# Moving a coupling cycle ahead of two expert steps in a pipelined decoder kernel

## The chip, the cores and the metric

The kernel runs on one core of one Trainium2 chip. The time is device microseconds (us) of one execution; of several runs the median is given. Lower is better.

## What is computed

The reference runs 32 sequences of 256 tokens of width 256 through six sublayers. Each adds its result to its input and takes a layer norm, and each reads the output of the one before:

```python
x = _layernorm(x + _L0_attn_ref(x, ...))        # random features, exp
x = _layernorm(x + _L0_xattn_ref(x, ctx, ...))  # cross attention, 16 heads, 120 keys
x = _layernorm(x + _L0_ffn_ref(x, ...))         # three coupling cycles
x = _layernorm(x + _L1_attn_ref(x, ...))        # state-space scan, 512 channels x 16 states
x = _layernorm(x + _L1_xattn_ref(x, ctx, ...))  # gated, gelu
x = _layernorm(x + _L1_ffn_ref(x, ...))         # 8 experts, the best one is taken
```

The two sublayers that matter here are the third and the sixth. The third is a small network with gelu that yields a gate for each token, and the gate turns the token's vector; this is done three times, the second cycle on the result of the first:

```python
for _ in range(NUM_CYCLES):
    tf = _coupling_net(out, ...)           # three gelu layers and a sigmoid
    combined = 0.7 * gf + 0.3 * tf         # gf: the same for a whole sequence
    coupling = BASE_COUPLING + adaptive_range * (combined - 0.5) * 2.0
    out = out + coupling * _twist(out)
```

In the sixth, the kernel lets all eight experts compute each token and adds the results with weights, of which all but one are zero.

## The kernel before

Two sequences, 512 tokens, make a group; there are 16. The kernel is a pipeline written out by hand: for each engine there is one list of work for a **turn**, and in a turn four groups are at different places. `f` is in the front part (sublayers 1 to 3), `m` in the scan of sublayer 4, `b` in the back part (5 and 6), and `nxt` is the one whose first sublayer and keys are made ready. 18 turns run: two that fill, 13 in a loop with all four groups present, one without `nxt`, one with `m` and `b` alone, and one with `b` alone. An engine works its list strictly in the order in which it stands in `turn` (TensorE) or `turn_` (VectorE, ScalarE, GpSimd, called POOL in the profile), so an instruction that waits holds up all that stands behind it on its engine.

**The coupling cycles.** `cycle(f, s)` on TensorE issues layers 1 to 4 for the two sequences of the group (the first layers of cycle 0 are issued just ahead of it by `layer(f, 1, 0)` and `layer(f, 1, 1)`, with the steps of the small global network, `glob`, between). ScalarE applies a gelu behind each layer (L1416, L1420, L1424) and the gate (L1430), after it has loaded the table for gelu (L1498). VectorE's `rotate` (L1038 to L1043) turns the vectors with the gate, and the next cycle's first layers wait for that. Layer 1 of cycle 0 waits for the copies of the second norm, which ScalarE makes in `copy_and_sum` (L1372).

**The experts.** `experts(b, s0, s1)` on TensorE issues expert steps `s`; a step is one block of 128 tokens through two experts: a 128x512 result in PSUM bank `MB[s % 2]`. `combine(b, s0, s1)` on VectorE (L1199) adds the results: for each pair of steps four sums, expert one of both blocks, then expert two of both. There are 16 steps. Since they use only two banks, step `s` waits until both sums of step `s - 2` are done:

```python
if s >= 2:
    pe.wait_ge(expert_added.sem, expert_added.at(g, added_after(s - 2)))
```

Steps 0 and 1 wait for the start of the sum. On its side a sum waits for its step's matmuls.

**The scan.** 64 scans (16 states for each of four chunks of channels; L1087) run on VectorE, with four outputs between (L1093). `states(m, n)` advances this list to entry `n`; scan 33, the first of the third chunk, is entry 34. ScalarE makes the decays for the scans (`decays`, L1479), at most 12 ahead of VectorE; POOL adds the states (L1671). At the first scan of a chunk VectorE also waits for a square that ScalarE makes (L1474).

`keys(nxt, f)` and `values(nxt, f)` on TensorE prepare the next group's attention; VectorE's `values` adds their bias (L982).

TensorE's matmuls are recorded under the line of one helper, L535 (transposes: L413 and L719), so the operands tell them apart: `w_expert_w,x45T` is an expert step, `x12T,w_cn_w` layer 1 of a cycle, `spare,w_cn_w` layers 2 to 4, `g,w_gc_w` the global network. A float32 matmul is recorded twice, so a step of two matmuls counts x4.

Of the kernel before, what the change touches and what calls it, by code (L numbers as in the profile page):

```python
# [136 lines left out]
def program(nc, ins, out):  # L137
    nc.disable_value_cache = True
    with ExitStack() as ctx:
# [293 lines left out]
        def added_after(s):  # L433


            return 4 * (s // 2) + 3 + s % 2
# [96 lines left out]
        def _(pe):  # L533
# [261 lines left out]
            def experts(g, s0, s1):  # L795

                for s in range(s0, s1):
                    pair, t = s // NT, s % NT
                    if s >= 2:

                        pe.wait_ge(expert_added.sem, expert_added.at(g, added_after(s - 2)))
                    else:
                        pe.wait_ge(acc_start.sem, acc_start.at(g, 2))
                    for c in range(DC):
                        last = mm(MB[s % 2][:, :], n5.xT[:, c, t * P:(t + 1) * P],
                                  expert_w[:, c, pair * 2 * D:(pair + 1) * 2 * D], c == 0, c == DC - 1)
                    last.then_inc(expert_ready.sem, 1)
# [10 lines left out]
            def turn(f, m, b, nxt):  # L818
# [66 lines left out]
                    experts(b, 0, 2)  # L885
                if f is not None:
                    norm_turn(pe, n2, f, TURN)
                if b is not None:
                    experts(b, 2, 4)
                if f is not None:  # L890
                    layer(f, 1, 0)
                    glob(f, 1)
# [6 lines left out]
                    keys(nxt, f)  # L899
                    values(nxt, f)  # L900
                if b is not None:
                    experts(b, 4, 9)
                if f is not None:
                    cycle(f, NB)
                if b is not None:
# [23 lines left out]
            with pe.Fori(0, G - 3) as i:  # L929
                turn((i, 2), (i, 1), (i, 0), (i, 3))  # L930
# [6 lines left out]
        def _(v):  # L937
# [160 lines left out]
            def states(g, upto):  # L1098

                if g is None:  # L1100
                    return
                if scanned.n is None:
                    scanned.start(v, g)
                while scanned.n < upto:
                    step(g, *PLAN[scanned.n])
                if upto == len(PLAN):
                    scanned.end()
                    scanned.n = None
# [74 lines left out]
            def combine(g, s0, s1):  # L1183

                for s2 in range(s0 // 2, s1 // 2):
                    pair, t0 = s2 // 2, s2 % 2 * 2
                    for e in range(2):
                        for t in (t0, t0 + 1):
                            s = pair * NT + t
                            done = 4 * s2 + 2 * e + (t - t0)  # L1190
                            if e == 0:
                                v.wait_ge(expert_ready.sem, expert_ready.at(g, s + 1))

                            if e:
                                v.wait_ge(expert_added.sem, expert_added.at(g, done - 1))
                            elif pair:
                                v.wait_ge(expert_added.sem, expert_added.at(g, done - 5))
                            x = 2 * pair + e
                            v.scalar_tensor_tensor(out=acc[:, t, :], in0=MB[s % 2][:, e * D:(e + 1) * D],  # L1199
                                                   scalar=weight[:, t, x:x + 1], in1=acc[:, t, :], op0=ALU.mult,  # L1200
                                                   op1=ALU.add).then_inc(expert_added.sem, 1)
# [21 lines left out]
            def turn_(f, m, b, nxt):  # L1223
# [44 lines left out]
                    norm_apply(v, n2, f)  # L1268
                if b is not None:
                    combine(b, 0, 2)  # L1270
                states(m, 30)
                if b is not None:
                    combine(b, 2, 4)
                states(m, 32)
                if f is not None:
                    global_base(f)
                    rotate(f, 0)
                    rotate(f, 1)
                states(m, 34)
                if b is not None:  # L1280
                    combine(b, 4, 6)
                states(m, 36)
# [490 lines left out]
```

## Time and profile before

| | |
|---|---|
| median of 3 runs | 3106.39 us (3101.62 to 3107.36) |
| profiled execution | 3099.29 us |
| its span, first to last instruction | 3097.5 us |
| mean granted TensorE clock | 0.872 |
| TensorE matmuls busy | 82% |
| VectorE busy | 81% |
| ScalarE busy | 56% |
| POOL busy | 48% |

The profile is of one execution. A line of its timeline has the start, the busy time, the engine and the source line, what is written from what, and how many instructions were merged into the line; in brackets stands how long the engine was idle just before and which instruction ended that. Merged instructions overlap a little, so the start of the next line is the better measure of how far one has come. Ends of matmuls are modelled.

### The profile page before, as it was taken

Reading aid. Unit: us, or ns where it says so; the run is one execution under the profiler, and the core shown is the slowest. Engines: PE = TensorE matmul, PEld = TensorE weight load, DVE = VectorE, ACT = ScalarE, POOL = GpSimd, SP = SyncE. Lnnn points to the kernel's source line nnn. Section 1 sums busy time; section 2 is a strip of 40 time slices with the busy share of each in tenths; the row PEclk is TensorE's granted clock in tenths of the full one; section 3 lists DMA queues with packets and bytes.
Section 4 is the critical chain, followed back from the end, with each engine's and each line's share of the span. In section 5 each row is a group of like instructions: output and inputs, shape, how many; then the busy total and the mean of one; then the engine's idle time right before and its main releaser. Section 6 shows DMA issues by size and latency. Waiting matters only on the chain.

```text
span 3097.5 us, 41602 instructions
## 1 busy us (share of the span) xinstructions
PE 2540.1 (82%) x11020; PEld 1469.9 (47%) x11020; DVE 2495.3 (81%) x4288; ACT 1727.8 (56%) x3062; POOL 1487.4 (48%) x1159
## 2 busy tenths in 40 slices
PE   6896888979888897888988788888888889887556
PEld 3544554544444454445545444554544445454323
DVE  2368888897978889898888978788897888978783
ACT  1457564646657474665646466564656646465620
POOL 1046354554535455563545545354553545456460
PEclk7868888888989989999898899898898989978687
DMA  3000000000000000000000000000000000000000
GB/s 131 10 8 10 14 11 14 17 14 7 10 21 10 14 17 14 7 10 21 10 14 13 18 7 10 21 10 14 13 3 21 10 14 7 7 7 1 14 7 7
DMA packets 16849, 45.72 MB, mean 15 GB/s; under 512 B 2248, under 2 KB 7056, under 8 KB 16400
## 3 DMA queue, kind: packets, MB, share of 16 engines
q1 hardware_dynamic: 16656, 43.96, 4.2%
q14 instruction: 171, 1.40, 0.2%
q8 instruction: 22, 0.36, 0.1%
HBM read 35.57 MB, written 8.39 MB: 14 GB/s over the span
## 4 chain that ended last, share of the span: by engine, by line
PE 47%; DVE 28%; issue 14%; ACT 7%; DVEq 2%; POOL 1%; ACTq 0%; DMA 0%; SPq 0%; POOLq 0%
PE bank L535 45%; DVE h_ring L1087 14%; DVE x L1199 3%; DVE ln_stats L387 2%; DVE smax L991 1%; POOL ysum L1671 1%; ACT a_ring L1479 1%; DVE x L405 1%; DVE xpad L1093 1%; PE bank L413 1%; DVE soft L1066 1%; ACT L1485 1%; ACT L1339 1%; DVE ln_mv L391 1%; ACT spare L1420 1%
## 5 line engine op out<-in xcount | busy, mean ns | idle before, releaser
L1671 POOL TENSOR_TENSOR ysum<-ysum,h_ring 128x512 f32<-128x512 f32 x896 | 1155.2, 1289 | 633.3 <-DVE h_ring L1087 571.3
L1087 DVE TENSOR_TENSOR_SCAN h_ring<-a_ring,bank 128x512 f32<-128x512 f32 x1024 | 1172.7, 1200 | 27.2 <-ACT bank L1474 16.2
L1479 ACT ACTIVATE a_ring<-soft,decay 128x510 f32<-128x510 f32 x1024 | 675.7, 717 | 198.4 <-DVE h_ring L1087 198.0
L535 PE MATMUL bank<-w_expert_w,x45T 128*128 128x512 f32 x1024 | 541.1, 675 | 199.0 <-DVE x L1199 191.4
L535 PEld LDWEIGHTS bank<-w_expert_w,x45T 128*128 128x128 f32 x1024 | 213.2, 216 | 490.9 <-DVE x L1199 253.5
L1658 POOL TENSOR_TENSOR soft<-xc,soft 128x512 f32<-128x512 f32 x64 | 81.0, 1276 | 655.2 <-ACT soft L1457 655.2
L535 PE MATMUL bank<-x3T,w_winT 128*128 128x512 f32 x512 | 291.0, 704 | 39.7 <-ACT x3T L419 31.4
L991 DVE TENSOR_REDUCE smax<-bank 128x4 f32<-128x480 f32 x256 | 156.4, 652 | 143.1 <-PE bank L535 143.1
L535 PE MATMUL bank<-qT,kmask 32*120 32x256 f32 x1024 | 207.2, 497 | 50.2 <-ACT spare L1386 40.6
L535 PE MATMUL bank<-spare,w_cn_w 128*128 128x256 f32 x768 | 217.7, 408 | 37.0 <-ACT spare L1416 22.4
L1199 DVE SCALAR_TENSOR_TENSOR x<-bank,weight,x 128x256 f32<-128x256 f32 x512 | 212.5, 474 | 40.4 <-PE bank L535 40.4
L398 ACT ACTIVATE ln_logv<-ln_mv,eps 128x4 f32<-128x4 f32 x96 | 28.3, 295 | 330.5 <-DVE ln_mv L391 252.7
L535 PE MATMUL bank<-kmask,qT 32*128 32x240 f32 x1024 | 151.8, 417 | 46.1 <-DVE smax L991 45.2
L1386 ACT ACTIVATE spare<-bank 120x512 f32<-120x512 f32 x256 | 138.4, 593 | 81.5 <-PE bank L535 81.4
L535 PEld LDWEIGHTS bank<-x3T,w_winT 128*128 128x128 f32 x512 | 104.3, 220 | 165.1 <-issue 111.5
L535 PEld LDWEIGHTS bank<-spare,w_cn_w 128*128 128x128 f32 x768 | 131.8, 193 | 105.7 <-ACT spare L1416 37.3
L535 PE MATMUL bank<-x12T,w_cn_w 128*128 128x256 f32 x768 | 180.0, 384 | 2.3 <-ACT x12T L1372 2.3
L1671 POOL TENSOR_TENSOR ysum<-h_ring 128x512 f32<-128x512 f32 x64 | 81.3, 1270 | 197.5 <-DVE h_ring L1087 197.5
L413 PE MATMUL bank<-w_ident,x 128*128 128x128 f32 x640 | 127.4, 322 | 49.6 <-DVE x L405 45.6
L535 PEld LDWEIGHTS bank<-x12T,w_cn_w 128*128 128x128 f32 x768 | 146.0, 192 | 40.3 <-issue 20.1
L1416 ACT ACTIVATE spare<-bank,w_columns 128x256 f32<-128x256 f32 x192 | 80.5, 472 | 139.6 <-PE bank L535 139.3
L535 PEld LDWEIGHTS bank<-kmask,qT 32*128 32x128 f32 x1024 | 94.9, 198 | 129.5 <-DVE smax L991 83.8
(149 smaller groups left out, 3890.2 us busy)
## 6 DMA issues: line engine op xcount, KB each, us to landing
x0T<-in_xT SPq DMA_DIRECT2D x16, 512.0 KB, 3.3
x<-in_x SPq DMA_DIRECT2D x16, 512.0 KB, 4.3
out<-x SPq DMA_DIRECT2D x16, 512.0 KB, 3.0
ctxT<-in_ctxT SPq DMA_DIRECT2D x16, 240.0 KB, 2.5
ctxTb<-in_ctxT SPq DMA_DIRECT2D x16, 240.0 KB, 2.7
ctxb<-in_ctx SPq DMA_DIRECT2D x16, 240.0 KB, 3.0
w_expert_w<-in_expert_w SPq DMA_DIRECT2D x1, 2048.0 KB
w_winT<-in_winT SPq DMA_DIRECT2D x1, 1024.0 KB
```

The source lines that it names most:

```text
L387: n.chain.then(v.bn_stats(n.stats[:, t, :], n.sum[:, t, :]))
L391: last = v.bn_aggr(n.mv[:, t, :], n.stats[:, t, :])
L413: last = pe.transpose(banks[c][:, t * P:(t + 1) * P], n.x[:, t, c * P:(c + 1) * P], ident[:, :])
L535: return pe.matmul(o, l, r, start=start, stop=stop)
L991: v.tensor_reduce(smax[:, t, :].rearrange("p (e r h) -> p r e h", e=DC, r=4)[:, r, :, :], bank[u % 3][:, 0:480].rearrange("p (e h k) -> p ...
L1087: scanned.then(v.tensor_tensor_scan(h_ring[:, k % HRING, :], a_ring[:, k % RING, :, :].rearrange("p b s -> p (b s)"), xc2, 0.0, ALU.mult, ...
L1199: v.scalar_tensor_tensor(out=acc[:, t, :], in0=MB[s % 2][:, e * D:(e + 1) * D], scalar=weight[:, t, x:x + 1], in1=acc[:, t, :], op0=ALU.mu ...
L1386: a.activation(probs[:, s % 4, :, :].rearrange("p k s -> p (k s)"), bank[s % 3][0:KEYS, :], ACT.Exp, scale=1.0 / np.sqrt(DK)).then_inc(pro ...
L1416: a.activation(h1[:, b, r, :], bank[b][:, r * S:(r + 1) * S], ACT.Gelu, bias=col("cn_b1", r)).then_inc(l1_ready.sem, 1)
L1479: a.activation(a_ring[:, k % RING, :, 1:S], delta[:, c, :].rearrange("p (b s) -> p b s", b=NB)[:, :, 1:S], ACT.Exp, scale=decay[:, k:k + 1 ...
L1658: p.tensor_tensor(out=delta[:, c, :], in0=xc[:, c, :], in1=soft[:, c, :], op=ALU.add)\
L1671: p.tensor_tensor(out=total, in0=first, in1=h_ring[:, k % HRING, :], op=ALU.add)\
```

## The change

On TensorE expert steps 2 and 3 no longer stand between the transposes of the second norm and the first layers of cycle 0. They are issued behind cycle 0 and the next group's keys and values, in one run with steps 4 to 8. On VectorE the four sums of steps 2 and 3 move from behind scan-list entry 30 to behind entry 34, which stands behind the rotations of cycle 0; the sums of steps 4 and 5 then follow behind entry 35 instead of directly behind entry 34. Entries 31 and 32 follow entry 30 without a break. No instruction is added or removed, and the lists of ScalarE, POOL and the DMA queue are as they were.

```diff
@@ TensorE, turn @@
                 if f is not None:
                     norm_turn(pe, n2, f, TURN)
-                if b is not None:
-                    experts(b, 2, 4)
                 if f is not None:
                     layer(f, 1, 0)
                     glob(f, 1)
...
                     keys(nxt, f)
                     values(nxt, f)
                 if b is not None:
-                    experts(b, 4, 9)
+                    experts(b, 2, 9)
                 if f is not None:
                     cycle(f, NB)
@@ VectorE, turn_ @@
                 if b is not None:
                     combine(b, 0, 2)
-                states(m, 30)
-                if b is not None:
-                    combine(b, 2, 4)
                 states(m, 32)
                 if f is not None:
                     global_base(f)
                     rotate(f, 0)
                     rotate(f, 1)
                 states(m, 34)
+                if b is not None:
+                    combine(b, 2, 4)
+                states(m, 35)
                 if b is not None:
                     combine(b, 4, 6)
                 states(m, 36)
```

## Rows read from the trace of the kernel before

**Rows 1.** The page: span, and busy time of each engine.
```profile
span 3097.5 us, 41602 instructions
...
PE 2540.1 (82%) x11020; PEld 1469.9 (47%) x11020; DVE 2495.3 (81%) x4288; ACT 1727.8 (56%) x3062; POOL 1487.4 (48%) x1159
```

**Rows 2.** Chain of waits, 1494 to 1545 us: start, length (both us), who.
```profile
1500.93 10.25 PE bank L535 x40
...
1536.37 0.42 DVE couple L1038
```

**Rows 3.** Timeline of TensorE, turn around 1500 us: start, us, line, operands, count.
```profile
1500.93 3.70 PE L535 MATMUL bank<-w_expert_w,x45T 128*128 128x512 f32 x8 [0.38 <-DVE x L1199]
...
1508.46 0.28 PE L535 MATMUL bank<-g,w_gc_w 128*64 128x2 f32 x2
1508.67 1.13 PE L535 MATMUL bank<-spare,w_cn_w 128*128 128x256 f32 x4
...
1516.88 3.60 PE L535 MATMUL bank<-w_expert_w,x45T 128*128 128x512 f32 x8
1521.77 3.70 PE L535 MATMUL bank<-w_expert_w,x45T 128*128 128x512 f32 x8 [1.30 <-DVE x L1199]
1526.54 1.98 PE L535 MATMUL bank<-w_expert_w,x45T 128*128 128x512 f32 x4 [1.07 <-DVE x L1199]
```

**Rows 4.** Timeline of ScalarE in the same turn.
```profile
1501.56 3.78 ACT L1479 ACTIVATE a_ring<-soft,decay 128x510 f32<-128x510 f32 x6
1505.36 1.28 ACT L1498 ACT_TABLE_LOAD   x1
1506.65 0.84 ACT L1416 ACTIVATE spare<-bank,w_columns 128x256 f32<-128x256 f32 x2
1507.38 0.26 ACT L1400 ACTIVATE g<-bank,w_columns 128x2 f32<-128x2 f32 x1
1508.57 0.84 ACT L1416 ACTIVATE spare<-bank,w_columns 128x256 f32<-128x256 f32 x2 [0.92 <-PE bank L535]
```

**Rows 5.** Timeline of VectorE in the same turn.
```profile
1506.75 1.64 DVE L1199 SCALAR_TENSOR_TENSOR x<-bank,weight,x 128x256 f32<-128x256 f32 x4
...
1513.41 0.41 DVE L1038 TENSOR_SCALAR couple<-gate,gate_scale,base 128x256 f32<-128x256 f32 x1 [2.44 <-ACT gate L1430]
...
1519.34 1.22 DVE L1087 TENSOR_TENSOR_SCAN h_ring<-a_ring,bank 128x512 f32<-128x512 f32 x1 [0.88 <-ACT bank L1474]
1520.48 1.63 DVE L1199 SCALAR_TENSOR_TENSOR x<-bank,weight,x 128x256 f32<-128x256 f32 x4
...
1525.61 1.27 DVE L1199 SCALAR_TENSOR_TENSOR x<-bank,weight,x 128x256 f32<-128x256 f32 x3 [0.22 <-PE bank L535]
1526.79 2.32 DVE L1087 TENSOR_TENSOR_SCAN h_ring<-a_ring,bank 128x512 f32<-128x512 f32 x2
...
1536.37 0.41 DVE L1038 TENSOR_SCALAR couple<-gate,gate_scale,base 128x256 f32<-128x256 f32 x1 [0.80 <-ACT gate L1430]
```

**Rows 6.** VectorE in other turns; engines and clock (PEclk, after POOL) in two stretches.
```profile
1335.34 0.41 DVE L1038 TENSOR_SCALAR couple<-gate,gate_scale,base 128x256 f32<-128x256 f32 x1 [2.44 <-ACT gate L1430]
...
1699.54 0.41 DVE L1038 TENSOR_SCALAR couple<-gate,gate_scale,base 128x256 f32<-128x256 f32 x1 [2.44 <-ACT gate L1430]
...
410.00:448.00 38.00, 34.97 (x123) 21.15 (x121) 32.22 (x52) 29.10 (x58) 19.57 (x16) 1.00 0.06 21
...
2593.00:2631.00 38.00, 34.97 (x123) 21.32 (x122) 32.22 (x52) 28.70 (x58) 19.25 (x15) 1.00 0.00 0
```

**Rows 7.** Timeline of TensorE: pairs of expert steps after stops, last turns.
```profile
2801.23 6.05 PE L535 MATMUL bank<-w_expert_w,x45T 128*128 128x512 f32 x8 [4.50 <-DVE x L1199]
...
2954.79 5.40 PE L535 MATMUL bank<-w_expert_w,x45T 128*128 128x512 f32 x8 [3.42 <-DVE x L1199]
...
2984.64 3.70 PE L535 MATMUL bank<-w_expert_w,x45T 128*128 128x512 f32 x8 [2.73 <-DVE x L1199]
```

**Rows 8.** Timeline of ScalarE in the first turn behind the loop.
```profile
2788.17 0.84 ACT L1416 ACTIVATE spare<-bank,w_columns 128x256 f32<-128x256 f32 x2 [0.60 <-PE bank L535]
```

## The prediction

> **What bounds the kernel now.** I read the page first: TensorE is busy for 82% and VectorE for 81% of the span [rows 1], so neither share settles anything. The order of work repeats every turn (some 180 us), so I took the turn around 1500 us and read its chain of waits: from 1500.93 to 1536.37 us the chain runs almost wholly through TensorE, with short visits to ScalarE and VectorE [rows 2]. It ends at the rotation of the second cycle, which VectorE waits for. From there VectorE works nearly without a gap to the end of the turn, so what delays that rotation delays the turn, and the next one starts behind it. So I followed the stretch engine by engine.
>
> In that stretch VectorE is idle four times: 2.44 us before the first rotation, 0.88 us before scan 33 of the list, 0.22 us before the second sum of the pair of expert steps 6 and 7, and 0.80 us before the second rotation, 4.34 us in all [rows 5]. The same waits stand in all 13 loop turns, to within 0.01 us; the first rotation of two more turns is shown [rows 6]. One turn can thus be worked out and multiplied.
>
> **The change part by part.**
> *What is removed at the old place.* Expert steps 2 and 3 (the "third and fourth") are eight matmuls, 3.70 us on TensorE from 1500.93 us [rows 3]. Their four sums are one 1.64 us group at 1506.75 us, 1.55 us up to the next scan [rows 5]. Taking the sums out there wins nothing: VectorE then meets its 2.44 us wait for the first gate 1.55 us earlier and waits longer. No transfer moves, and nothing moves past anything on SP's or POOL's queue.
>
> *What the first cycle gains.* The copies of the second norm end about when ScalarE turns to its decays, 1501.56 us [rows 4]; the first layer can start then instead of after the two expert steps, some 2.7 us earlier. But ScalarE is not there yet: six decays (3.78 us) and a table load stand ahead of the first gelu, which starts at 1506.65 us with no wait [rows 4]. It cannot move. Only the second gelu can: it waits 0.92 us for TensorE [rows 4]. Without that wait the next limit is TensorE's second layer of the small global network, which needs the activation that starts at 1507.38 us and takes 0.26 us [rows 4]; so it starts at about 1507.70 instead of 1508.46 us, and layer 2 behind it at 1507.91 instead of 1508.67 us [rows 3]. **The whole first cycle, and with it the rotation, the keys and the values, comes 0.76 us earlier.** Bounds: nothing (if TensorE keeps its place) and 0.92 us (the whole wait). I take 0.76, as the row that becomes late next is in the trace.
>
> A rule to weigh here: the row puts the next gelu 1.29 us after the start of the table load. The Trainium skill (ScalarE: Activation LUTs, What ACT_TABLE_LOAD costs) counts about 2.66 us for a switch, a drain included; by it the first gelu would come at about 1508.0 us, the gain would be nil and the sum some 10 us larger. This trace disagrees with the page, and I go by the row.
>
> *What is added behind the cycle.* TensorE now issues steps 2 to 8 in one row where it issued 4 to 8. All use two PSUM banks: step s waits for both sums of step s-2. So TensorE and VectorE take turns, and a pair has a period that the trace shows: step 6 starts at 1521.77, step 8 at 1526.54 us, 4.77 us, of which 3.70 us are matmuls and 1.07 us the wait for VectorE [rows 3]. From the first pair to the second it is 1521.77 - 1516.88 = 4.89 us. In the old order steps 4 and 5 found their banks long free, as the sums of 2 and 3 had been done before the rotation. In the new order steps 4 and 5 must wait for those sums.
>
> Laid out: values end 0.76 us earlier, so step 2 starts at 1516.12 us. The scan before the sums shifts from 1519.34 to 1518.58 us, so the moved sums start at 1519.72 us (old: the next pair's at 1520.48 us [rows 5]) and just meet the end of step 3. Step 4 starts 1.29 us after that, 1521.01 us; step 6 at 1525.78, step 8 at 1530.55 us, against 1526.54 us before. **One more period of 4.77 less the 0.76 gained: 4.01 us later.**
>
> VectorE agrees. Its old wait of 0.22 us at the second sum of a pair becomes a wait at both later pairs, since between two pairs it has only its sums (1.55 us) and one scan (1.2 us) against 4.77 us, at the last pair also the value copies. The scan behind the pair of steps 6 and 7 moves from 1526.79 [rows 5] to about 1530.80 us. The second cycle stands behind step 8 on TensorE, and ScalarE's last decay ahead of that cycle needs that very scan; both come 4.0 us later, so the 0.80 us wait stays as it is and the second rotation starts at about 1540.4 us.
>
> *What hides it afterwards.* Nothing that I find: the later waits of TensorE are for VectorE, and ScalarE's and POOL's hang on scans; all move along. What is queued behind the waiting step 4 on TensorE is steps 5 to 8 and the whole second cycle; behind VectorE's waiting sums stand all later scans.
>
> *The two turns behind the loop.* The first has no next input, so no keys and values; its second gelu waits only 0.60 us [rows 8], so the gain is 0.76 - 0.32 = 0.44 and the loss 4.33 us. The second has no front part and no cycle: the sums move behind scan 33 and this arrives 1.55 us earlier, but one more period follows and starts cold, since TensorE then has stood for over 8 us. The nearest rows for a pair after a long stop are 5.40 us (3.42 us stop) and 6.05 us (4.50 us stop) [rows 7], against 3.60 us [rows 3]: 4.77 + 1.80 - 1.55 = 5.0 us, or 5.7 by the other row. I take 5.0. The first two turns and the last have the same order in effect.
>
> *The sum.* 13 x 4.01 = 52.1, with 4.3 and 5.0: 61.4 us. The profiled execution took 3099.29 us; with the change about 3160.7. The median of the runs is 7.1 us higher, so on that scale 3167.8; I say 3166.
>
> The bounds: without any gain 13 x 4.77 and the two turns, 71 us; with the full 0.92 us 59 us. The clock outside the stretch differs from turn to turn anyhow (the first rotation, at 1335.34, 1513.41 and 1699.54 us, shows turns of 178.1 and 186.1 us [rows 5, 6]), and every later stage now falls elsewhere in that pattern: I allow 15 us down and 25 us up for it.
>
> **The rivals.**
> *A, my forecast: one more turnaround of the two banks in each turn.* 3166 us, chance 0.73.
>
> *B, the clock falls as well.* Over the stretch the granted clock is 1.00 (2.4 GHz) in all 13 turns, first and last shown [rows 6]; the waits of 1.30 and 1.07 us between pairs do not lower it, nor does one of 2.73 us, while pairs after stops of 3.42 and 4.50 us run slow [rows 7]. The new order adds stops of about 1.2 us ahead of the first layer and 2 us ahead of the global network's second layer, with thin matmuls behind. If the clock falls there or among the pairs, a pair's surplus of 1.80 us is the price: 13 x 1.8 = 23 us more, 3189 us. Chance 0.15. Where it fell in this trace the stops were longer, so it is not the likeliest. The Trainium skill (TensorE: Matmul & The Clock Gate, A second HAM failure mode: psum-queue depth-cycling) says that short stops between groups of matmuls, as a kernel cycles through PSUM banks, can make the clock swing; by that rule this case holds, and the 13 turns at 1.00 speak against it.
>
> *C, faster.* The mechanism is the same handover at the two banks. If VectorE had enough of its own between two pairs, the turnaround would cost nothing and the 0.76 us would stay: 14 x 0.76 = 11 us, 3096 us. It decides at 4.77 us of scans and sums between pairs; the new list has some 2.7 and 3.4 us. Only a much shorter handover than the row's would do it. Chance 0.06.
>
> *D, no change.* VectorE falls 4 us behind but a later wait takes it up, for instance that for the transposes at the end of the turn. This gives 3106 us. Against it: those waits follow VectorE's own rotation and shift with it. Chance 0.06.
>
> **How the numbers follow.** The likeliest is A, 3166. A and B hold 0.88; the range from 3145 to 3200 takes in A with its bounds and most of B, and leaves out C and D (0.12) and the tails. About 0.2% (6 us) is what a measurement of this kernel can tell from no change. Faster 0.06 (C), within it 0.06 (D), slower 0.88 (A, B).
>
> **What the new profile would show.** Right: in every loop turn the wait before the first rotation grows to about 3.2 us and this starts 0.76 us nearer to the sums of steps 0 and 1; step 4 waits about 1.3 us behind step 3, and two waits of about 1.07 us follow; VectorE waits for TensorE some 1.5 to 2 us at each of the pairs 4/5 and 6/7; the second rotation comes about 4.0 us later behind the sums of steps 0 and 1; the granted clock there is 1.00. Wrong: if the first gelu starts earlier, the gain is larger; if pairs run at 5.40 us, it is B; if the pairs' waits on VectorE are missing, C; if the second rotation is late but the turn is not longer, D.

## The result, and the profile after

The changed kernel takes **3179.93 us** (median of 4 runs, 3177.15 to 3184.8) against 3105.53 us beside it: ratio 1.0249, 95% interval 1.0234 to 1.0265, 74.4 us slower. The profiled execution took 3179.07 us, 79.8 us more than that of before.

The page of the changed kernel: span, busy time of each engine (x instructions), and the group of the expert sums (busy time, mean ns | idle time ahead of it and what ended it). VectorE's lines are two lower than before: the sums are L1197, the rotation L1036, the scan L1085.

```profile
span 3177.3 us, 41602 instructions
...
PE 2602.1 (82%) x11020; PEld 1492.1 (47%) x11020; DVE 2504.4 (79%) x4288; ACT 1727.9 (54%) x3062; POOL 1487.4 (47%) x1159
...
L1197 DVE SCALAR_TENSOR_TENSOR x<-bank,weight,x 128x256 f32<-128x256 f32 x512 | 214.4, 474 | 85.3 <-PE bank L535 85.2
```

The same group on the page of the kernel before:

```profile
L1199 DVE SCALAR_TENSOR_TENSOR x<-bank,weight,x 128x256 f32<-128x256 f32 x512 | 212.5, 474 | 40.4 <-PE bank L535 40.4
```

The number of instructions is the same, 41602, and the shares of busy time hardly move [rows 1]. Two things moved: VectorE's sums now stand idle for 85.3 us, nearly all of it waiting for TensorE, where it was 40.4 us; and TensorE is busy 62 us longer, at a mean granted clock of 0.850 against 0.872.

TensorE in a turn of the loop, the timeline that answers to [rows 3] (start, us, line, operands, count, idle time before):

```profile
1540.61 1.99 PE L535 MATMUL bank<-x12T,w_cn_w 128*128 128x256 f32 x8 [1.22 <-ACT x12T L1370]
...
1546.56 0.28 PE L535 MATMUL bank<-g,w_gc_w 128*64 128x2 f32 x2 [1.78 <-ACT g L1398]
...
1548.34 4.69 PE L535 MATMUL bank<-spare,w_cn_w 128*128 128x256 f32 x12
1556.21 3.60 PE L535 MATMUL bank<-w_expert_w,x45T 128*128 128x512 f32 x8
1561.42 3.70 PE L535 MATMUL bank<-w_expert_w,x45T 128*128 128x512 f32 x8 [1.61 <-DVE x L1197]
1566.19 3.70 PE L535 MATMUL bank<-w_expert_w,x45T 128*128 128x512 f32 x8 [1.06 <-DVE x L1197]
1570.95 1.99 PE L535 MATMUL bank<-w_expert_w,x45T 128*128 128x512 f32 x4 [1.06 <-DVE x L1197]
```

Two things stand here. Steps 2 to 8 are the last four rows: three handovers of the banks where [rows 3] has two, 4.77 us from the second pair to the third and 4.76 us on to step 8. And the twelve matmuls of layers 2 to 4 at 1548.34 us take 4.69 us. The stretches of that turn (us, busy time of PE, PEld, DVE, ACT, POOL, then the granted clock, DMA share, GB/s):

```profile
1546.75:1553.75 7.00, 6.93 (x25) 5.02 (x25) 2.50 (x5) 3.91 (x11) 3.79 (x3) 0.76 0.00 0
1553.75:1580.75 27.00, 22.93 (x73) 12.93 (x72) 22.13 (x35) 16.45 (x28) 12.77 (x10) 1.00 0.03 10
```

Behind the stops of 1.22 and 1.78 us the granted clock of layers 2 to 4 is 0.76: for part of that time TensorE ran at the lower of its two levels. In the old order the same stretch stood at 1.00 in every loop turn ([rows 6] shows the first and the last). ScalarE and VectorE in the same turn, the timelines that answer to [rows 4] and [rows 5]:

```profile
1544.22 1.28 ACT L1496 ACT_TABLE_LOAD   x1
1545.52 0.84 ACT L1414 ACTIVATE spare<-bank,w_columns 128x256 f32<-128x256 f32 x2
...
1546.39 0.85 ACT L1414 ACTIVATE spare<-bank,w_columns 128x256 f32<-128x256 f32 x2
```

```profile
1538.48 1.65 DVE L1197 SCALAR_TENSOR_TENSOR x<-bank,weight,x 128x256 f32<-128x256 f32 x4
...
1553.08 0.41 DVE L1036 TENSOR_SCALAR couple<-gate,gate_scale,base 128x256 f32<-128x256 f32 x1 [3.64 <-ACT gate L1428]
...
1565.26 1.27 DVE L1197 SCALAR_TENSOR_TENSOR x<-bank,weight,x 128x256 f32<-128x256 f32 x3 [1.23 <-PE bank L535]
...
1570.02 1.27 DVE L1197 SCALAR_TENSOR_TENSOR x<-bank,weight,x 128x256 f32<-128x256 f32 x3 [1.23 <-PE bank L535]
...
1580.78 0.41 DVE L1036 TENSOR_SCALAR couple<-gate,gate_scale,base 128x256 f32<-128x256 f32 x1 [0.80 <-ACT gate L1428]
```

From the first rotation to the second it is now 1580.78 - 1553.08 = 27.70 us, against 22.96 us [rows 5].

**Where the 79.8 us are.** I divide a loop turn on VectorE by four marks: S1 from the sums of steps 0 and 1 to the first rotation, S2 to the second rotation, S3 to the third, and the rest up to the next turn's sums of steps 0 and 1. The table has the means over the 13 loop turns, each from the timelines as above, for all kernels of this study; "three" is S1 + S2 + S3, and the last two columns compare 13 times its difference from before (without the rest) with the measured difference of the medians. The table is from one execution of each, which lay 9 us above its median for bank3, 17 us above for before_b3, 9 us below for decays_b3 and 6 us below for the kernel before, and within 5 us for the others:

| kernel | S1 | S2 | S3 | three | rest | 13 x difference | medians |
|---|---|---|---|---|---|---|---|
| before | 13.80 | 22.95 | 41.20 | 77.95 | 103.75 | | |
| after | 14.48 | 27.70 | 41.20 | 83.37 | 103.88 | +70.5 | +74.4 |
| fill2 | 13.03 | 27.70 | 41.20 | 81.93 | 106.13 | +51.8 | +88.9 |
| fill4 | 13.15 | 27.71 | 41.20 | 82.06 | 106.52 | +53.4 | +103.7 |
| sums_late | 13.80 | 29.98 | 41.20 | 84.98 | 103.88 | +91.4 | +95.2 |
| sums_order | 14.41 | 25.48 | 42.73 | 82.61 | 104.66 | +60.6 | +67.5 |
| decays | 11.17 | 29.58 | 41.18 | 81.93 | 103.50 | +51.8 | +51.7 |
| bank3 | 14.50 | 23.87 | 42.08 | 80.45 | 103.35 | +32.5 | +20.2 |
| before_b3 | 13.80 | 21.75 | 42.07 | 77.62 | 105.92 | -4.3 | -0.3 |
| decays_b3 | 11.18 | 24.61 | 42.07 | 77.86 | 103.14 | -1.1 | -3.0 |
| reorder | 11.18 | 23.54 | 41.79 | 76.51 | 104.40 | -18.7 | -11.8 |
| reorder_so | 11.18 | 23.96 | 43.10 | 78.23 | 104.95 | +3.7 | -1.9 |

For the changed kernel: 61.7 us in S2 (13 x 4.75), 8.8 us in S1 (13 x 0.68), 1.7 us in the rest, 6.3 us behind the loop's last turn and 1.3 us ahead of its first make the 79.8 us.

### The profile page after: what moved, and what is told of

It is laid out like the page before. It is cut to its first block, busy times and chain, and to the rows that moved or that the text cites. A ratio compares the mean times of both kernels' runs of the same rounds, so it can differ in the third digit from the quotient of the medians.

```text
span 3177.3 us, 41602 instructions
## 1 busy us (share of the span) xinstructions
PE 2602.1 (82%) x11020; PEld 1492.1 (47%) x11020; DVE 2504.4 (79%) x4288; ACT 1727.9 (54%) x3062; POOL 1487.4 (47%) x1159
## 4 chain that ended last, share of the span: by engine, by line
PE 44%; DVE 29%; issue 15%; ACT 8%; DVEq 2%; POOL 2%; ACTq 0%; DMA 0%; POOLq 0%; SPq 0%
PE bank L535 42%; DVE h_ring L1085 14%; DVE x L1197 3%; DVE ln_stats L387 2%; POOL ysum L1669 1%; DVE smax L989 1%; ACT a_ring L1477 1%; PE bank L413 1%; DVE xpad L1091 1%; DVE soft L1064 1%; DVE qT L1039 1%; ACT L1337 1%; DVE couple L1036 1%; DVE x L405 1%; DVE x12T L1041 1%
## 5 line engine op out<-in xcount | busy, mean ns | idle before, releaser
L1085 DVE TENSOR_TENSOR_SCAN h_ring<-a_ring,bank 128x512 f32<-128x512 f32 x1024 | 1173.0, 1199 | 26.9 <-ACT bank L1472 15.9
L535 PE MATMUL bank<-w_expert_w,x45T 128*128 128x512 f32 x1024 | 552.6, 687 | 209.2 <-DVE x L1197 201.6
L535 PE MATMUL bank<-x3T,w_winT 128*128 128x512 f32 x512 | 306.9, 738 | 38.7 <-ACT x3T L419 30.3
L1197 DVE SCALAR_TENSOR_TENSOR x<-bank,weight,x 128x256 f32<-128x256 f32 x512 | 214.4, 474 | 85.3 <-PE bank L535 85.2
L535 PE MATMUL bank<-spare,w_cn_w 128*128 128x256 f32 x768 | 234.7, 436 | 34.2 <-ACT spare L1414 22.4
L535 PE MATMUL bank<-qT,kmask 32*120 32x256 f32 x1024 | 215.1, 513 | 47.7 <-ACT spare L1384 39.1
L535 PEld LDWEIGHTS bank<-spare,w_cn_w 128*128 128x128 f32 x768 | 143.0, 208 | 107.8 <-ACT spare L1414 37.2
L535 PEld LDWEIGHTS bank<-qT,kmask 32*120 32x120 f32 x1024 | 98.0, 232 | 121.1 <-ACT spare L1384 83.7
```

The source lines that it names most:

```text
L535: return pe.matmul(o, l, r, start=start, stop=stop)
L1085: scanned.then(v.tensor_tensor_scan(h_ring[:, k % HRING, :], a_ring[:, k % RING, :, :].rearrange("p b s -> p (b s)"), xc2, 0.0, ALU.mult, ...
```

## The experiments

Each ratio is to the kernel before, run beside it on the same chip; a value under 1 is faster. The questions: is the handover the cost, is the fallen clock the cause of the missing gain, and what does each remedy bring?

**fill4 and fill2: TensorE kept busy ahead of the first cycle.** Where steps 2 and 3 stood, the changed kernel gets four or two more matmuls of 128x512, whose result nobody reads.

```diff
+            def filler(n):
+                for k in range(n):
+                    mm(bank[0][:, :], ident[:, :], expert_w[:, 0, 0:2 * D], True, True)
...
                     norm_turn(pe, n2, f, TURN)
+                if b is not None and f is not None:
+                    filler(4)
```

> The changed kernel with four matmuls of 128x512 that nobody reads, issued on TensorE where expert steps 2 and 3 stood, between the transposes of the second norm and the first layer of cycle 0. They cost TensorE 3.6 us and fill the two stops of 1.22 and 1.78 us that the change opened there. Theory (the clock): the missing gain of the change is the granted clock, which falls in the first cycle behind these stops; with the filler layers 2 to 4 of cycle 0 take 3.66 us again instead of 4.69 us, the first rotation comes some 0.4 us before its place in the kernel before instead of 0.8 us behind it, and 12 turns win 1.2 us: 3165 us. Rival (the first cycle is late for another reason, a wait or TensorE's own order): the filler wins nothing or delays further, 3180 us or more. The second rotation stays about 27.7 us behind the first by both.

> The changed kernel with two such matmuls as filler, 1.8 us, so that the layers start 1.8 us later than in the changed kernel but the network's activation, not TensorE, still sets layer 2 of cycle 0; one stop of about 1.3 us is left in place of 1.22 and 1.78 us. Theory (the clock): if one stop of this length doesn't lower it, the whole 0.76 us of the prediction appears, first rotation 1.55 us earlier than in the changed kernel, 12 x 1.55 = 19 us: 3161 us; if the clock still falls in some turns, between 3161 and 3180 us, by the number of these. Rival (another reason): 3180 us.

fill4 measured 3203.05 us, ratio 1.0342 (1.0299 to 1.0385); fill2 3188.25 us, 1.0286 (1.0246 to 1.0326). TensorE's timeline in fill2, from the first cycle to the end of a turn, and the clock of the two stretches (columns as above):

```profile
1558.08 3.66 PE L535 MATMUL bank<-spare,w_cn_w 128*128 128x256 f32 x12
...
1595.29 5.25 PE L535 MATMUL bank<-w_expert_w,x45T 128*128 128x512 f32 x8 [4.21 <-DVE x L1203]
...
1612.57 5.14 PE L535 MATMUL bank<-w_expert_w,x45T 128*128 128x512 f32 x8 [5.15 <-DVE x L1203]
...
1628.61 3.26 PE L535 MATMUL bank<-x,w_ident 128*128 128x512 f32 x4 [2.85 <-DVE x L1203]
```

```profile
1556.50:1563.50 7.00, 6.73 (x30) 5.08 (x31) 4.22 (x9) 4.94 (x11) 3.99 (x4) 1.00 0.00 0
1628.50:1640.50 12.00, 11.46 (x44) 8.29 (x44) 9.80 (x25) 0.00 (x0) 3.38 (x3) 0.86 0.00 0
```

The local claim holds: without the stop ahead of the first layer the clock is 1.00, layers 2 to 4 take 3.66 us, and S1 is 13.03 us in every loop turn, 0.77 us less than the 13.80 of before, where I had worked out 0.76. The claim on the whole time fails: neither kernel is faster than the changed one, and fill4 is clearly slower. The same place of the turn in the changed kernel, timeline and stretch:

```profile
1586.91 6.29 PE L535 MATMUL bank<-w_expert_w,x45T 128*128 128x512 f32 x8 [4.21 <-DVE x L1197]
...
1604.19 6.18 PE L535 MATMUL bank<-w_expert_w,x45T 128*128 128x512 f32 x8 [4.11 <-DVE x L1197]
...
1620.22 1.98 PE L535 MATMUL bank<-x,w_ident 128*128 128x512 f32 x4 [1.81 <-DVE x L1197]
```

```profile
1620.11:1632.11 12.00, 10.53 (x47) 7.99 (x47) 11.37 (x33) 1.60 (x7) 3.41 (x3) 1.00 0.00 1
```

With filler a pair behind the same stop of 4.21 us takes 5.25 instead of 6.29 us; TensorE then stands 5.15 instead of 4.11 us, is through the next pair in 5.14 instead of 6.18 us, and stands 2.85 instead of 1.81 us ahead of the residual at the end of the turn. There the four matmuls take 3.26 instead of 1.98 us, and VectorE waits for them: from the third rotation to the first norm statistics behind them it is 14.8 us in most turns instead of 13.1. Two turns need some 19 us there; in both TensorE stops twice ahead of transposes without a releaser, for 2.35 us in this row:

```profile
887.87 0.33 PE L719 MATMUL bank<-w_ident,x12T 128*128 128x128 f32 x1 [2.35 <-issue]
```

Together these are the longer rest (106.13 against 103.88 us). So the fall of the clock in the first cycle is the cause of the lost gain there, but with filler the clock falls in another place of the turn, where it costs as much or more. fill4, whose rest is 106.52 us, is not taken apart here.

**sums_late: the sums' new place alone.** TensorE's old order, VectorE's new one.

```diff
+                if b is not None:
+                    experts(b, 2, 4)
                 if f is not None:
                     layer(f, 1, 0)
...
-                    experts(b, 2, 9)
+                    experts(b, 4, 9)
```

> Half of the change alone: TensorE's order is that of the kernel before (steps 2 and 3 ahead of cycle 0), VectorE's is that of the changed one (their sums behind the first rotations). Theory (the handover): the clock holds in the first cycle and the first rotation stays in its old place, but step 4 must wait for the late sums, from 1516.9 to about 1521.8 us in the turn shown, 4.9 us; the pair starts cold (5.4 us and not 3.6) and the second rotation comes 6.6 us late: 3106 + 14 x 6.6 + 5 = 3203 us; 3175 us if the clock doesn't fall. Rival (the matmuls' new place on TensorE costs, the place of the sums is free): 3106 us.

3194.53 us, ratio 1.0307 (1.0261 to 1.0354). The first rotation stands in its old place (S1 13.80 us). S2 is 7.03 us longer than before. TensorE behind the values:

```profile
1572.40 6.09 PE L535 MATMUL bank<-w_expert_w,x45T 128*128 128x512 f32 x8 [4.71 <-DVE x L1199]
```

TensorE stands 4.71 us for the sums that now come behind the rotation, and runs the pair behind that stop in 6.09 us. So the place of the sums costs on its own; that steps 2 and 3 go along on TensorE makes it cheaper, not dearer, since they fill that stop (the three stretches take 83.37 against 84.98 us).

**bank3: a third PSUM bank.** Steps 4 and 7 of the changed kernel write to bank 5 once the global network has left it, so steps 2 to 4 find their banks free, and each of steps 5 to 8 waits for the sums three steps back instead of two.

```diff
+        EB = [MB[0], MB[1], MB[0], MB[1], bank[5], MB[0], MB[1], bank[5], MB[0]] + [MB[k % 2] for k in range(9, 16)]
+        BEFORE = {s: s - 2 for s in range(2, 16)}
+        BEFORE.update({5: 2, 6: 3, 7: 4, 8: 5})
...
-                        pe.wait_ge(expert_added.sem, expert_added.at(g, added_after(s - 2)))
+                        pe.wait_ge(expert_added.sem, expert_added.at(g, added_after(BEFORE[s])))
```

> The changed kernel with a third PSUM bank for expert steps 4 and 7, so that steps 2 to 8 go round three banks and no step waits for the sums directly before it. Theory (the handover of two banks costs 4.77 us a turn): step 4 follows step 3 without a stop, the waits of TensorE of 1.61, 1.06 and 1.06 us go or shrink, the second rotation follows the first by some 24 to 25 us instead of 27.7, and a turn costs about 1.9 us more than in the kernel before instead of 5.5: 3136 us. Rival (it is the 3.6 us of matmuls of steps 2 and 3, now issued between the two cycles, that push the second cycle back): a third bank changes nothing, 3175 to 3180 us.

3119.57 us, ratio 1.0071 (1.0046 to 1.0096): some 54 us of the 74 come back. TensorE's and VectorE's timelines:

```profile
1531.35 4.98 PE L539 MATMUL bank<-spare,w_cn_w 128*128 128x256 f32 x12
...
1536.05 0.41 DVE L1042 TENSOR_SCALAR couple<-gate,gate_scale,base 128x256 f32<-128x256 f32 x1 [3.40 <-ACT gate L1434]
...
1539.51 12.18 PE L539 MATMUL bank<-w_expert_w,x45T 128*128 128x512 f32 x28
...
1559.99 1.26 DVE L1042 TENSOR_SCALAR couple<-gate,gate_scale,base 128x256 f32<-128x256 f32 x1
```

The seven steps are one row without a stop, 28 records in 12.18 us. S2 falls to 23.87 us. The first cycle still runs slow (4.98 us), and S1 is as in the changed kernel. What is left above the kernel before is 0.70 us in S1, 0.92 us in S2 and 0.88 us in S3; decays_b3 below shows where the last two come from.

**before_b3: the same third bank in the old order**, the control: is a third bank simply good? The two tables of bank3 in the kernel before, and:

```diff
-                    experts(b, 4, 9)
+                    experts(b, 4, 9, f)
```

> The old order with the same third PSUM bank for steps 4 and 7. It asks whether the third bank is a gain of its own, or only takes back what the change added. Theory (the extra period of the two banks is what the change costs, and the third bank took just that back): in the old order TensorE's waits of 1.30 and 1.07 us between the pairs vanish, but VectorE, which sets the pace, waited only 0.22 us for them and 0.80 us at the second rotation, so at most 13 x 1.0 us are to be had: 3089 to 3103 us, from the first to the second rotation 22.0 to 22.9 us (22.95 without). Rival (the third bank is worth the same 60 us in any order, so its run said nothing about the change): some 3042 us, and the stretch is 4 us shorter.

3097.63 us, ratio 0.9997 (0.9979 to 1.0015): nothing. VectorE's first two rotations and TensorE's steps 4 to 8 between them:

```profile
1531.42 0.41 DVE L1044 TENSOR_SCALAR couple<-gate,gate_scale,base 128x256 f32<-128x256 f32 x1 [2.44 <-ACT gate L1436]
...
1534.88 8.75 PE L539 MATMUL bank<-w_expert_w,x45T 128*128 128x512 f32 x20
...
1553.17 1.25 DVE L1044 TENSOR_SCALAR couple<-gate,gate_scale,base 128x256 f32<-128x256 f32 x1
```

The stops between the pairs are gone here too, S2 is 1.20 us shorter and S3 0.87 us longer: the second rotation no longer waits, but its first instruction takes 1.25 us instead of 0.41 [rows 5]. So the old order had almost nothing to win from the bank, while the new order won 54 us: what the bank took away was the handover that the change had added.

**sums_order: the bank freed by the first two sums.** In the changed kernel the four sums of a pair go block by block instead of expert by expert.

```diff
-                    for e in range(2):
-                        for t in (t0, t0 + 1):
+                    for t in (t0, t0 + 1):
+                        for e in range(2):
```

> The changed kernel with the four sums of a pair in another order: both experts of the first block, then both of the second, so that a step's bank is free after two sums and not after three, and the step behind can start while its neighbour is still computed. Two sums of a pair now wait for the one directly before them, about 0.1 us each. Theory (the handover of the two banks): the two waits of 1.06 us in the row of steps 2 to 8 go, the one ahead of step 4 stays, the second rotation follows the first by some 25.4 us instead of 27.7: 3150 us. Rival (the matmuls moved behind the first cycle cost, not the handover): 27.7 us as before, 3180 us or a little more for the extra waits.

3169.56 us, ratio 1.0212 (1.0183 to 1.0241). S2 falls to 25.48 us, as expected, which confirms the handover in a second way: a bank that comes back after two sums shortens it. But a sum now waits for the one directly ahead of it:

```profile
1561.82 1.89 DVE L1197 SCALAR_TENSOR_TENSOR x<-bank,weight,x 128x256 f32<-128x256 f32 x4
```

Four sums take 1.89 instead of 1.64 us. S3, with four such groups, grows by 1.53 us: 1.0 us from the sums, and 0.5 us because the second rotation's first instruction takes 0.90 instead of 0.41 us. Of the 2.2 us won in S2 0.7 is left behind S3.

**decays: ScalarE's decays cut ahead of the first cycle.** My working said that ScalarE's six decays hold the first gelu. The changed kernel with four fewer of them there:

```diff
-SQUARE_AT = (0, 18, 38, 59)
+SQUARE_AT = (0, 18, 34, 59)
...
-                decays(m, 36)
+                decays(m, 32)
                 if f is not None:
                     cycle(f, 0)
```

> The changed kernel with ScalarE brought forward: four of the six decays ahead of cycle 0 are made behind it (32 and not 36 ahead of the cycle), and the square for the third chunk comes four decays earlier. TensorE and VectorE as in the changed kernel. Theory (ScalarE's decays and table load, not TensorE, held the first gelu, so that the change could win 0.76 us at most): the first gelu comes about 2.5 us earlier, the stop of 1.78 us on TensorE in front of the global network's second layer goes, the first rotation comes some 2.9 us before its place in the kernel before, and a turn costs one handover less this, about 2 us: 3140 us; 3160 us if the clock falls in the first cycle all the same. Rival (ScalarE was not what held the cycle): the first rotation stays where it is, 3180 us.

3153.79 us, ratio 1.0159 (1.013 to 1.0188). VectorE, ScalarE and TensorE in order of time:

```profile
1534.09 1.65 DVE L1197 SCALAR_TENSOR_TENSOR x<-bank,weight,x 128x256 f32<-128x256 f32 x4
...
1537.39 1.28 ACT L1496 ACT_TABLE_LOAD   x1
1538.69 0.84 ACT L1414 ACTIVATE spare<-bank,w_columns 128x256 f32<-128x256 f32 x2
...
1541.89 3.66 PE L535 MATMUL bank<-spare,w_cn_w 128*128 128x256 f32 x12
...
1545.27 1.26 DVE L1036 TENSOR_SCALAR couple<-gate,gate_scale,base 128x256 f32<-128x256 f32 x1 [1.55 <-ACT gate L1428]
...
1554.45 5.40 PE L535 MATMUL bank<-w_expert_w,x45T 128*128 128x512 f32 x8 [2.12 <-DVE x L1197]
```

The first gelu comes at 1538.69 us, 4.60 us behind the sums of steps 0 and 1 (7.04 in the changed kernel), the stop of 1.78 us ahead of the global network's second layer is gone, the first cycle is at full clock, and the first rotation follows the sums after 11.18 us. Part of it is given back: TensorE, ready earlier, stands 2.12 instead of 1.61 us for the sums of steps 2 and 3 and runs the pair behind that in 5.40 us, so S2 is 30.23 us in 8 turns. In the other five it is 28.53 us, 0.83 us more than in the changed kernel, since the first rotation's first instruction takes 1.26 us instead of 0.41 (in all 13 turns).

**decays_b3: both remedies at once.** The edits of decays and of bank3.

```diff
-                decays(m, 36)
+                decays(m, 32)
...
-                    experts(b, 2, 9)
+                    experts(b, 2, 9, f)
```

> The changed kernel with both remedies: ScalarE's decays ahead of the first cycle cut from entry 36 to 32 (square at 34), and the third bank for steps 4 and 7. Theory (two separate losses, ScalarE's place in the first cycle and the banks' handover): from the sums of steps 0 and 1 to the first rotation 11.2 us as with the earlier decays alone, from the first to the second rotation about 24 us as with the third bank alone; the turn is 3.4 us shorter than with the third bank alone, 3119.6 - 13 x 3.4 = 3075 us. Rival (the turn is held elsewhere by then: VectorE has no idle time left in the stretch, as in the order that starts steps 2 and 3 behind the first cycle, which took 3090 us): 3085 to 3095 us, the second stretch longer than 24 us or the end of the turn longer.

3094.93 us, ratio 0.9991 (0.9974 to 1.0009), some 20 us above what I expected of two independent losses. VectorE:

```profile
1510.54 1.26 DVE L1042 TENSOR_SCALAR couple<-gate,gate_scale,base 128x256 f32<-128x256 f32 x1 [1.55 <-ACT gate L1434]
...
1521.85 1.27 DVE L1203 SCALAR_TENSOR_TENSOR x<-bank,weight,x 128x256 f32<-128x256 f32 x3 [0.28 <-PE bank L539]
...
1535.16 1.25 DVE L1042 TENSOR_SCALAR couple<-gate,gate_scale,base 128x256 f32<-128x256 f32 x1
```

S1 is 3.32 us shorter than with the bank alone, but S2 is 0.74 us longer. VectorE waits 1.55 us ahead of the first rotation, 0.86 us ahead of scan 33, 0.28 us at a sum, and not at all at the second rotation: 2.69 us a turn against 4.34 us before. But both rotations now begin with an instruction of 1.25 us, where the kernel before has 0.41 us [rows 5]. POOL's timeline at the second one:

```profile
1534.99 1.27 POOL L1675 TENSOR_TENSOR ysum<-ysum,h_ring 128x512 f32<-128x512 f32 x1
```

The rotation's instruction starts 0.17 us behind the start of this addition and ends 0.15 us behind its end, and so it is in all 13 turns and at both rotations, to within 0.01 us. In the kernel before the first rotation starts while POOL does not add, and the second starts near the end of an addition. The two longer instructions, 0.84 us each, take back the 1.65 us of waits that were won; the move of the sums of steps 2 and 3, 1.55 us, from S1 into S2 is the other part of the longer S2. The three stretches together are within 0.09 us of before: the two remedies take back the whole cost of the change, and no more. The rival's view, that the turn is then held elsewhere, has the better of it. That POOL's addition holds the instruction is read from these times; no run moves the addition.

**reorder: the idea in another order.** From the changed kernel: steps 2 and 3 directly behind the first cycle, ahead of keys and values; their sums behind the first scan that follows the rotation; three scans, or the value copies and two scans, between the pairs of sums; step 8 behind the second cycle; the first decays as above, and four fewer ahead of the second cycle. TensorE's part of the edit:

```diff
                     cycle(f, 0)
+                if b is not None:
+                    experts(b, 2, 4)
                 if nxt is not None:
                     keys(nxt, f)
                     values(nxt, f)
                 if b is not None:
-                    experts(b, 2, 9)
+                    experts(b, 4, 8)
                 if f is not None:
                     cycle(f, NB)
                 if b is not None:
-                    experts(b, 9, 12)
+                    experts(b, 8, 12)
```

> A version meant to keep the idea and avoid its cost: steps 2 and 3 directly behind cycle 0 but ahead of keys and values, so that their sums are done (behind the first rotations, between scans 32 and 33) before step 4 is due; step 8 behind the second cycle; ScalarE makes 32 decays ahead of cycle 0 and 44 ahead of cycle 1; the sums of 4 and 5 behind entry 36, those of 6 and 7 behind entry 38 of the scan list. Theory (handover and ScalarE's place are the two causes): no long wait ahead of step 4, the second rotation some 2.7 us earlier in the turn than in the kernel before: 3068 us, 3090 us if the clock falls in the first cycle. Rival (any expert steps behind the first cycle delay the second): above 3106 us.

3090.34 us, ratio 0.9961 (0.9939 to 0.9983): faster than both kernels, 11.8 us faster than the one before, less than half of what I expected. VectorE:

```profile
1518.35 1.63 DVE L1199 SCALAR_TENSOR_TENSOR x<-bank,weight,x 128x256 f32<-128x256 f32 x4
1519.90 3.43 DVE L1087 TENSOR_TENSOR_SCAN h_ring<-a_ring,bank 128x512 f32<-128x512 f32 x3
1523.25 1.63 DVE L1199 SCALAR_TENSOR_TENSOR x<-bank,weight,x 128x256 f32<-128x256 f32 x4
...
1528.38 1.27 DVE L1199 SCALAR_TENSOR_TENSOR x<-bank,weight,x 128x256 f32<-128x256 f32 x3 [0.22 <-PE bank L535]
```

Between the first two pairs of sums VectorE now has three scans, and its waits in S2 are 0.22 and 0.20 us. The handover is covered by VectorE's own work, as rival C of the prediction wanted it; S1 is 2.6 us shorter. S2 and S3 are each 0.59 us longer and the rest 0.65 us, which leaves about 0.8 us a turn of it. S2 has 1.55 us of sums more than before and, as in decays_b3, a first rotation that begins with 1.26 instead of 0.41 us, against 1.48 us less of waits and an output (L1093) of 0.74 instead of 0.96 us; S3 begins with 0.97 instead of 0.41 us.

**reorder_so: the same with the sums block by block.**

```diff
-                    for e in range(2):
-                        for t in (t0, t0 + 1):
+                    for t in (t0, t0 + 1):
+                        for e in range(2):
```

> The version before with the other order of the sums too (a step's bank is free after two sums). Theory: the handovers of 1.06 us that are left between the pairs go as well, at the price of 0.2 us of waits a pair on VectorE, 1.6 us a turn in 8 pairs; between 10 us faster and 15 us slower than the version before, 3058 to 3083 us. Rival: no handover is left on the way that sets the end, and only the price shows, some 20 us slower than that version.

3100.23 us, ratio 0.9994 (0.9972 to 1.0016). With no handover left to shorten only the price shows, 1.31 us in S3 (1.0 us of it from four groups of chained sums, 0.3 us from the second rotation's first instruction, 1.25 against 0.97 us), and the gain of reorder is gone.

## Why the prediction was right, and where its sum was not

The time lies in the range, and the direction and the main mechanism were right: one more turnaround of the two banks. What came is A together with a fall of the clock as in B; it lies inside the range, which was drawn to take in A's bounds and most of B. The central sum was 18.4 us too low against the profiled execution (61.4 us against 79.8). Step by step:

- **The added period.** Worked out: 4.77 us from the gain's new place on, so S2 27.7 us. Measured 27.70 in all 13 turns, 4.75 us longer. The single rows agree as well: waits of 1.06 us ahead of the later pairs. VectorE waits 1.23 us for each of them in the rows shown (and 0.65 us more for the pair of steps 4 and 5), where I had 1.5 to 2 us. Step 4's stop is 1.61 instead of 1.3 us, because step 2 starts only 3.13 us behind the late first rotation, where step 4 had started 3.47 us behind it [rows 3, 5]; the sums come 7.04 us behind the rotation, as before (7.07), so the second rotation is not later for it. bank3 and before_b3 together show that this is the handover and not something else: the bank that removes it brings 54 us in the new order and nothing in the old one.
- **No wait swallows it.** The rest of the turn is 103.88 us against 103.75 in the mean (single turns of before lie between 99.9 and 108.2 us). VectorE does stand there, unlike what the prediction says of the end of the turn, for example 5.00 us for ScalarE at 1644.67 us of the changed kernel, but these waits come later by as much. Rival D, no change, has nothing for it.
- **The first cycle's gain: the step that failed.** "The whole first cycle, and with it the rotation, the keys and the values, comes 0.76 us earlier." Up to layer 2 it does: the first gelu starts without a wait behind the table load, the second at 1546.39 us without one too, the global network's second layer 0.32 us behind its activation's start, and layer 2 1.25 us behind the first gelu, as worked out. Then the clock falls, and from layer 2 to the rotation it takes 1553.08 - 1546.77 = 6.31 us instead of 4.74 us [rows 3, 5]. The gain of 0.76 becomes a loss of 0.80 us, 0.68 us in the mean of the turns. Over 13 turns the difference to my sum is 13 x (0.76 + 0.68) = 18.7 us; the other terms cancel to -0.3 us (S2 -0.3, the rest +1.7, behind the loop -3.0, ahead of it +1.3).

One turn of the changed kernel shows what the step had in mind. VectorE and TensorE there, and the clock of that stretch:

```profile
789.32 1.66 DVE L1197 SCALAR_TENSOR_TENSOR x<-bank,weight,x 128x256 f32<-128x256 f32 x4
...
797.40 0.28 PE L535 MATMUL bank<-g,w_gc_w 128*64 128x2 f32 x2 [1.78 <-ACT g L1398]
...
798.98 3.66 PE L535 MATMUL bank<-spare,w_cn_w 128*128 128x256 f32 x12
...
802.36 0.41 DVE L1036 TENSOR_SCALAR couple<-gate,gate_scale,base 128x256 f32<-128x256 f32 x1 [2.07 <-ACT gate L1428]
```

```profile
792.74:799.74 7.00, 5.21 (x28) 4.09 (x27) 6.33 (x7) 6.06 (x13) 6.61 (x6) 1.00 0.00 0
```

13.04 us from the sums to the rotation, against 13.80: the 0.76. The same stop of 1.78 us stands there, and one of 1.22 us ahead of the first layer as in the other turn, and the clock held: these stops don't bring it down each time.

- **Rival B** was half right. I had named both stops as places where the clock could fall, and gave it 0.15; it fell behind the second of them, at 1.56 us a turn where I had 1.8, while the pairs of experts ran at full clock. I held it unlikely because the waits between pairs had not lowered the clock in the old order, waits up to 2.73 us long [rows 7]. Those were single stops between full pairs; here two stand close together with thin matmuls between. fill2 removes the first of the two (one of 1.55 us is left) and the clock holds; decays removes the second (one of 1.18 us is left) and it holds as well; bank3 keeps both, and S1 is 14.36 us or more in all 13 turns. What the thin matmuls add is not tried by itself. The rule of the Trainium skill that I had set aside (TensorE: Matmul & The Clock Gate, A second HAM failure mode: psum-queue depth-cycling) is about short stops while a kernel cycles through PSUM banks. Of the stops of this kind here the short ones, 1.61 and 1.06 us between the pairs, left the clock at 1.00; the two stops behind which it fell to 0.76 wait for ScalarE (L1370 and L1398), not for a bank.
- **The table load.** The gelu starts 1545.52 - 1544.22 = 1.30 us behind the start of the load, so the row was the right price. The 2.66 us of the Trainium skill (ScalarE: Activation LUTs, What ACT_TABLE_LOAD costs) are a load of about 1283 ns and a drain of about 1380 ns; the row agrees with the load, 1.28 us, and no row here shows the drain. The prediction had held the row of the load against the sum of both.
- **The turns behind the loop.** 9.3 us worked out, 6.3 measured from the first sum of the turn behind the loop to the end: 4.45 us up to the second rotation (4.33 worked out), 4.64 us in the second turn behind the loop, that of the added period (5.0 worked out), less 2.79 us between, which I had not foreseen. In that second turn the pair behind the longer stop (8.64 us) ran in 6.33 us, slower than both of my rows.

## What to carry to other kernels

When work is moved behind a dependency, follow the buffers that it held: here steps that had found their PSUM banks free paid a whole turnaround in the new order, and a third bank, tried in both orders, shows it. A gap that costs nothing on the path can still lower the clock of what follows, so a new stop is to be priced with the slower clock, above all where another stop stands close by. And a gain on one engine is worth no more than what the next one leaves: in reorder the earlier gelu brought 2.6 us at the first rotation and 0.8 us a turn in the end.

## What the runs showed of the hardware that I had not expected

Work given to TensorE to hold its clock moved the fall instead of removing it: fill2 won 1.45 us a turn in the first cycle (S1) and lost 2.25 us in the rest. The rows show a chain of pairs that alternately run faster and leave a longer stop. In the loop turns of the kernel before, the changed one and fill2 the four matmuls of the residual took 1.98 us behind stops of up to 2.38 us, and 2.44 us or more behind stops of 2.59 us or more; whether the length of this stop decides was not tried by itself, and a pair of steps ran in its full-clock time, 3.70 us, behind 2.73 us [rows 7].

The first instruction of a rotation on VectorE takes 0.41 us when POOL does not add meanwhile. Where it starts early in one of POOL's additions it ends 0.15 us behind that addition and takes 1.25 or 1.26 us: at the second rotation of bank3 and before_b3, at the first of decays, and at both of decays_b3, in all 13 turns. So a wait of VectorE's that was removed came back here as a longer instruction.

Left open: why the clock held in one turn of the changed kernel; what the stops marked "issue" ahead of transposes in the two filler kernels are (2.35 us in the row above, where the trace names no releaser; no other kernel of this study has them); and why reorder's rest is 0.65 us longer than before.
